# Shifting the state-space inputs by one row: matrix products, or a trip through DRAM

## What is computed

```python
# second token mixer (state space), inside the two-layer network; DIM=512, D_INNER=1024, NHEADS=16, D_STATE=64, CHUNK=64
def ssd_chunk(X, A, Bm, Cm):
    ...                       # S_t = exp(A_t) S_{t-1} + B_t X_t,  Y_t = C_t S_t, written chunk by chunk
zxBCdt = x @ fq4(W_in).T
z = zxBCdt[..., :D_INNER]
x_heads = jax.nn.silu(x_conv).reshape(Bsz, L, NHEADS, HEADDIM)
dt = jax.nn.softplus(dt_raw + dt_bias)
A_disc = -jnp.exp(A_log)[None, None, :] * dt
...                           # rmsnorm, bias and rotation of Bm and Cm
lam = jax.nn.sigmoid(x @ fq4(W_lambda).T)
gamma = lam * dt
beta = (1.0 - lam) * dt * jnp.exp(A_disc)
X = x_heads * gamma[..., None] + jnp.pad(x_heads[:, :-1] * beta[:, 1:, :, None], ((0, 0), (1, 0), (0, 0), (0, 0)))
Y, _ = ssd_chunk(X, A_disc, Bm, Cm)
Y = Y + x_heads * D_param[:, None]
Y = Y.reshape(Bsz, L, D_INNER) * jax.nn.silu(z)
return rmsnorm(Y) @ fq4(W_out).T
```

## Time and profile before

| | |
|---|---|
| median of 3 runs | 3940.6 us (3938.12 to 3940.74) |
| profiled execution | 3943.84 us, its span 3942.0 us |
| TensorE matmul busy | 3380.4 us (86%) |
| VectorE busy | 2652.5 us (67%) |
| ScalarE, GpSimd busy | 1180.4 us (30%), 502.9 us (13%) |
| mean granted TensorE clock | 0.917 of full speed |
| products with `shift` (1227) | 64 records, 32.9 us |
| products with `edge` (1229) | 48 records, 24.5 us |
| token loop of batch 1 | 2785.6 to 2906 us |

### The profile page before, as it was taken

One profiled execution on the slowest core, in us unless ns is written; L12 is line 12 of the kernel. 1 busy time (PEld: TensorE's weight loads), 2 busy tenths in 40 slices (PEclk: granted clock), 3 DMA queues, 4 the chain that ended last, 5 costly groups with the idle time before them and its releaser, 6 DMA issues.

```text
span 3942.0 us, 36808 instructions
## 1 busy us (share of the span) xinstructions
PE 3380.4 (86%) x12493; PEld 2058.3 (52%) x12493; DVE 2652.5 (67%) x3769; ACT 1180.4 (30%) x1948; POOL 502.9 (13%) x404
## 2 busy tenths in 40 slices
PE   1877877877878999999999778898889888988898
PEld 0553653643555777677777435543454346434643
DVE  6877778788785777888888254664566455645563
ACT  1332332332331445334334122212221223123310
POOL 1002002002003111111111112020212011201100
PEclk9888988988989999999999887899889988998799
DMA  3201211211203778787877510132013201220011
GB/s 137 81 24 43 80 34 38 84 34 35 76 23 115 251 246 273 228 275 241 267 269 250 218 53 33 75 112 86 32 75 112 86 32 75 92 106 32 7 58 43
DMA packets 276635, 436.66 MB, mean 111 GB/s; under 512 B 52320, under 2 KB 189536, under 8 KB 263904
## 3 DMA queue, kind: packets, MB, share of 16 engines
q1 hardware_dynamic: 256768, 379.85, 28.5%
q0 software_dynamic: 19680, 54.46, 4.4%
HBM read 364.59 MB, written 93.77 MB: 116 GB/s over the span
## 4 chain that ended last, share of the span: by engine, by line
PE 59%; DVE 24%; DVEq 6%; ACT 5%; issue 3%; DMA 1%; POOL 1%; SPq 0%; ACTq 0%; POOLq 0%
PE bank L1019 11%; PE bank L1048 6%; PE bank L1287 6%; PE bank L1300 4%; PE bank L1308 4%; PE bank L835 3%; PE bank L1216 3%; PE bank L1156 3%; DVE sb_gla L1888 3%; PE bank L1194 2%; DVE sb_ratio L1863 2%; DVEq L1869 2%; PE bank L1025 2%; PE bank L815 2%; PE bank L1252 2%
## 5 line engine op out<-in xcount | busy, mean ns | idle before, releaser
L1019 PE MATMUL bank<-sb_xT,sb_work 128*128 128x256 f32 x2304 | 512.6, 382 | 1.6 <-issue 0.8
L1019 PEld LDWEIGHTS bank<-sb_xT,sb_work 128*128 128x128 f32 x2304 | 438.9, 192 | 75.1 <-issue 17.5
L835 PE MATMUL bank<-sb_gla,sb_work 128*128 128x256 f32 x896 | 261.1, 444 | 111.8 <-DVE sb_work L1890 99.2
L1048 PE MATMUL bank<-sb_work,sb_hT 128*128 128x512 f32 (+1 forms) x666 | 296.1, 592 | 0.0
L835 PEld LDWEIGHTS bank<-sb_gla,sb_work 128*128 128x128 f32 x896 | 189.6, 219 | 174.8 <-DVE sb_work L1890 120.1
L815 PE MATMUL bank<-sb_hT,sb_work 128*128 128x512 f32 x384 | 182.1, 622 | 99.0 <-DVE sb_hT L1837 99.0
L1300 PE MATMUL bank<-sb_parts,sb_gla 128*128 128x512 f32 x512 | 238.8, 610 | 4.5 <-ACT sb_gla L1632 4.1
L1308 PE MATMUL bank<-sb_parts,sb_gla 128*128 128x512 f32 x512 | 230.8, 593 | 6.3 <-DVE sb_work L2469 6.3
L1287 PE MATMUL bank<-sb_work,sb_parts 128*128 128x512 f32 x512 | 231.7, 612 | 2.7 <-ACT sb_work L1645 2.7
L1888 DVE TENSOR_TENSOR sb_gla<-sb_gla,sb_work 128x1024 f32<-128x1024 f32 x112 | 145.9, 1303 | 129.9 <-PE bank L835 124.4
L1156 PE MATMUL bank<-sb_parts,sb_hT 128*128 128x512 f32 x512 | 231.1, 611 | 0.0
(11 more groups left out here) (403 smaller groups left out, 5950.2 us busy)
## 6 DMA issues: line engine op xcount, KB each, us to landing
sb_work<-scratch_gu SPq DMA_DIRECT2D x63, 1408.0 KB
sb_parts<-scratch_mx SPq DMA_DIRECT2D x16, 3072.0 KB, 11.3
sb_work<-moe_w SPq DMA_DIRECT2D x63, 512.0 KB, 6.4
scratch_y<-sb_work SPq DMA_DIRECT2D x48, 512.0 KB, 7.4
sb_parts<-scratch_fq SPq DMA_DIRECT2D x24, 1024.0 KB, 8.0
sb_work<-w_qkvg SPq DMA_DIRECT2D x64, 256.0 KB, 2.4
scratch_gu<-moe_w SPq DMA_DIRECT2D x32, 512.0 KB, 5.8
sb_parts<-fT SPq DMA_DIRECT2D x48, 256.0 KB
```

The costliest lines, as they stand in the source:

```text
L835: mm = pe.matmul(dst.rearrange("p (h n l) -> p h n l", h=HPC, l=size), kS[u % 2][:, k * P:(k + 1) * P], late[:, :, k, :, 1, :], start=True ...
L1019: mm = pe.matmul(dst, egu[j % 3][:, which * NC + k, m * P:(m + 1) * P], xt[j % 2][:, k, :], start=(k == 0), stop=(k == NC - 1))
L1048: mm = pe.matmul(bank(YB[s]), einter[j % 2][0:n, a:a + P], edn[j % 3][0:n, m * D:(m + 1) * D], start=(m == 0), stop=(m == EC - 1))
```

## The change

The products with `shift` and `edge`, the two matrices and the wait for `s_y` ahead of them go. A DRAM tensor `d_late` of 1 + 512 rows is added, whose row 0 GpSimd zeroes once with a DMA at the start. In each batch SyncE stores each finished `xh[k]` one row further on (512 KB), waits for that to land, and loads rows k*128 to k*128+127 back (512 KB), which are the values of the token before; they come into `R[2]` and `R[1]`. These 8 transfers stand in SyncE's queue ahead of the feed-forward loads. VectorE waits once per batch, in tile 0, for all eight, multiplies `late[k]` by beta in place (one instruction of 1024 columns) and adds it.

```diff
--- before.py
+++ after.py
@@ -78,10 +78,6 @@
     parts["ident"] = eye
     parts["ones"] = np.ones((P, P))
     parts["avg_d"] = np.full((P, P), 1.0 / D)
-    parts["shift"] = np.eye(P, k=1)
-    edge = np.zeros((P, P))
-    edge[P - 1, 0] = 1.0
-    parts["edge"] = edge
     head = np.arange(P) // GK
     parts["own_head"] = (head[:, None] == head).astype(np.float32)
     for i in range(NLM):
@@ -146,6 +142,7 @@
     d_gu = nc.dram_tensor("scratch_gu", [NE, P, 2 * NC, EI], F32, kind="Internal").ap()
     d_ids = nc.dram_tensor("scratch_ids", [NE * CAP, 1], U, kind="Internal").ap()
     d_y = nc.dram_tensor("scratch_y", [NSLOT, D], F32, kind="Internal").ap()
+    d_late = nc.dram_tensor("scratch_late", [1 + T, DI], F32, kind="Internal").ap()
     ctx = ExitStack()
     with ctx:
         def sb(name, cols, parts=P):
@@ -351,7 +348,7 @@
         s_v, s_dt, s_cs, s_ang, s_bcn, s_rope, s_tmc, s_cst = series("s_set_dve", 8)
         s_xz = ev("s_xz", NT * 4)
         s_silu = ev("s_silu", NT * 4)
-        s_shift = ev("s_shift", NT)
+        s_late = ev("s_late", 2 * NT, 16)
         s_xg = ev("s_xg", NT)
         s_csb = ev("s_csb", NT * 4)
         s_diff = ev("s_diff", NT * 4)
@@ -492,6 +489,7 @@
 
         X2 = [R[0], xT]
         xb = R[1]
+        late = [R[2 - k // 2][:, (k % 2) * 1024:(k % 2 + 1) * 1024] for k in range(NT)]
         yg = [w(s * 512, 512) for s in range(4)] + [w(14144, 512), small2[:, 2048:2560]]
         yacc = [w(13120 + s * 512, 512) for s in range(2)]
         wzx = big[:, 0:8192].rearrange("p (m c o) -> p m c o", m=4, c=NC)
@@ -771,6 +769,13 @@
                     load_r3(b)
                     sp.wait_ge(x4_ready.sem, x4_ready.at(b - 1, NC))
                     sp.dma_start(out[b - 1], r3(X2[(b - 1) % 2][:, :], T)).then_inc(stored.sem, 16)
+
+                sp.wait_ge(h2_ready.sem, h2_ready.at(b, NT))
+                for k in range(NT):
+                    sp.wait_ge(s_silu.sem, s_silu.at(b, 4 * k + 2))
+                    sp.dma_start(d_late[1 + k * P:1 + (k + 1) * P, :], xh[k]).then_inc(s_late.sem, 16)
+                    sp.wait_ge(s_late.sem, s_late.at(b, 2 * k + 1))
+                    sp.dma_start(late[k], d_late[k * P:(k + 1) * P, :]).then_inc(s_late.sem, 16)
 
                 for ib in range(FB):
                     s = ib % 2
@@ -1220,14 +1225,6 @@
 
                 for k in range(NT):
                     t = slice(k * P, (k + 1) * P)
-                    if k:
-                        pe.wait_ge(s_y.sem, s_y.at(b, k))
-                    for h in range(2):
-                        col = slice(h * 512, (h + 1) * 512)
-                        mm = pe.matmul(bank(h), cst("shift"), xh[k][:, col], start=True, stop=(k == 0))
-                        if k:
-                            mm = pe.matmul(bank(h), cst("edge"), xh[k - 1][:, col], start=False, stop=True)
-                    mm.then_inc(s_shift.sem, 1)
                     if k:
                         pe.wait_ge(s_state.sem, s_state.at(b, k))
                     cs_bcast(k, 0)
@@ -1655,6 +1652,8 @@
                 pool.memset(x, 0.0)
             pool.drain()
             pool.dma_start(d_ids.rearrange("(p n) o -> p (n o)", p=P), zeros.bitcast(U)).then_inc(ids_zero.sem, 16)
+            pool.dma_start(d_late[0:1, :].rearrange("a (p n) -> (a p) n", n=zeros.shape[1]),
+                           zeros[0:DI // zeros.shape[1], :]).then_inc(ids_zero.sem, 16)
 
             for b in range(NB):
                 if b:
@@ -1671,7 +1670,7 @@
                         pool.wait_ge(g_d.sem, g_d.at(u - 1, 1))
                     pool.tensor_tensor(qk, qS[u % 2], kS[u % 2], ALU.mult).then_inc(g_pool.sem, 1)
                 if b == 0:
-                    pool.wait_ge(ids_zero.sem, 16)
+                    pool.wait_ge(ids_zero.sem, 32)
                 pool.wait_ge(m_slot.sem, m_slot.at(b, 1))
                 for i in range(NTK):
                     tk = b * NT + i // TOPK
@@ -2143,7 +2142,7 @@
                 route(b)
                 last = b == NB - 1
                 if b == 0:
-                    dve.wait_ge(ids_zero.sem, 16)
+                    dve.wait_ge(ids_zero.sem, 32)
                 for j in range(ST):
                     dve.wait_ge(m_silu.sem, m_silu.at(b, j + 1))
                     dve.wait_ge(m_up.sem, m_up.at(b, j + 1))
@@ -2398,13 +2397,12 @@
                     differences(0)
 
                     x = Xg[k % 2]
-                    dve.wait_ge(s_shift.sem, s_shift.at(b, k + 1))
-                    for h in range(2):
-                        tt(r3(Xd[:, h * 512:(h + 1) * 512], SP_), r3(bank(h), SP_),
-                           bcast(tm[:, k, 1, h * 8:(h + 1) * 8], SP_), ALU.mult)
+                    if k == 0:
+                        dve.wait_ge(s_late.sem, s_late.at(b + 1, 0))
+                    tt(r3(late[k], SP_), r3(late[k], SP_), bcast(tm[:, k, 1, :], SP_), ALU.mult)
                     dve.drain()
                     dve.wait_ge(s_gx.sem, s_gx.at(b, k + 1))
-                    tt(x, x, Xd, ALU.add).then_inc(s_xg.sem, 1)
+                    tt(x, x, late[k], ALU.add).then_inc(s_xg.sem, 1)
                     differences(1)
                     masked(0)
                     differences(2)
```

## The result

The changed kernel takes 3951.56 us (median of 8 runs, 3946.19 to 3957.27) against 3940.67 (8 runs, 3937.68 to 3949.44): a ratio of 1.0027, 95% interval 1.0016 to 1.0039. So it is slower by about 11 us, where 3938.2 and "no change" were forecast as likeliest. The profiled execution has a span of 3948.1 us and a mean granted clock of 0.912 (before: 3942.0 and 0.917). VectorE has 12 us more to do (2664.4 us) and TensorE 30 us less (3350.5 us), though 57 us of its products are gone: most of the difference is old work that now takes longer, as the next lines show.

A forecast was written before the change was run, and what follows sets the result against it. TensorE carries 59% of the span, but removed products count only where the next step waits for it. Terms of -0.6 us a batch, -2.4 in four, took 3940.6 to 3938.2 us; range 3925 to 3954.

The forecast's parts named there:

- What bounds, and which products are on the chain: Token loop: removed products count only where TensorE is waited for, so in tiles 0, 2 and 3, not tile 1.
- Tile 0, +0.39 from exclusion: Tile 0: VectorE's beta product with both inputs in SBUF and GpSimd exclude each other, losing 0.39 us.
- Tile 1, +1.24: Tile 1: removal gives 0, but TensorE's clock falls in the new pause and an out_project half takes 1.24 us more.
- Tiles 2 and 3, -1.12 each: Tiles 2 and 3: the exponential comes directly behind its table load and the clock holds, gaining 1.12 us a tile.
- Transfers at 0: The stores and loads of 512 KB land before VectorE can use the data, so they cost 0.
- Sum: Four token loops: +0.39 + 1.24 - 1.12 - 1.12 = -0.6 us a batch, -2.4 us in all.
- rival 2: Tiles 1 to 3: without the products each out_project begins at 1.2 GHz; +3 us a batch, +12, 3953; chance 0.12.
- Rival 3: Tile 0: the last load lands at 2792.9 or later, delaying product and addition 2.46 us; 3957 in all; chance 0.08.

The follow-up runs named there:

- experiment 4: Changed kernel plus two unread 512-column products behind the first broadcast of tiles 1 to 3: 3932.50 us, ratio 0.9978 to the kernel before.
- experiment 8: Changed kernel with early beta products and two unread products, minus each block's store and load: 3918.68 us, against 3916.94 with transfers.
- experiment 1: Kernel before with the 14 shift and edge products taken out and nothing in their place: 3951.65 us, ratio 1.0029.
- experiment 2: Changed kernel with as many unread products as before in their old place in tiles 1 to 3: 3945.32 us, ratio 1.0008 to the kernel before.
- experiment 6: Changed kernel with GpSimd's Dx in tile 0 moved after the two products that follow the addition: 3953.35 us, ratio 1.0035 to the kernel before.

## Why the prediction was wrong, step by step

- **What bounds, and which products are on the chain:** right. In tiles 2 and 3 the exponential moved directly behind its table load (2849.71 + 1.28, then 2851.01), and with the clock up (experiment 4) these tiles gained 1.13 us in the mean.
- **Tile 0, +0.39 from exclusion:** right. Measured +0.4 (once +0.7); the product took 1.97 us and `Dx` 2.88, where 1.9 and 2.8 had been named as signs. The Trainium skill's lock rule ("SBUF — State Buffer", "SBUF: two separate sides") is borne out once more: the product took 1.97 us and the addition 2.77, where such an instruction takes 1.23 alone.
- **Tile 1, +1.24:** right in kind, too small. It lost 1.9 to 2.0. `out_project` took 5.7 to 6.0 us, since the clock stayed at 1.2 GHz for most of it (in batch 1 until about 2827, 4.6 us after its start), and the transposes, said to have room, took 1.98 us and ended 0.1 us after the exponential. The row of 5.08 us that set the term was of a half that began at 1.2 GHz and got 2.4 GHz back sooner, after about 3.3 us (granted clock 0.50 in 2895 to 2898 of before, 0.72 in 2898 to 2901).
- **Tiles 2 and 3, -1.12 each:** this step failed: "TensorE's pause here is 2 us with full work on both sides; I let the clock hold, as in 2818 to 2821". There is no full work on both sides. In the changed kernel `out_project`'s second half is followed by 1.82 us of idle time, 1.10 us of transposes with broadcasts around them, and 1.03 us idle again, and TensorE is busy for 1.25 us of 2848 to 2851. The stretch 2818 to 2821 of before was busy for 1.78, with 3.4 us of `shift` and `edge` products a little ahead of it. The nearer row was 2824 to 2827 of before, busy for 1.22, behind which the clock fell; it was used for tile 1 only. Five of eight `out_project` halves came out at 5.8 to 6.3 us and three at 3.84, so in pauses of this kind the clock went either way; what decides between them is not shown. Instead of -9.0 these eight tiles gave -0.5 in sum. Where the clock held the forecast could come out to the digit: tile 2 of batch 3 is at 28.56 us against 29.69.
- **Transfers at 0:** right, shown by experiment 8. In batch 1 of the changed kernel the last load lands 3.5 us after its issue at 2784.16, ahead of VectorE's product at 2789.25.
- **Sum:** 2.0 in tiles 0, 7.8 in tiles 1 and -0.5 in tiles 2 and 3 are +9.2, against -2.4. It is rival 2 in its mechanism and nearly in its price (+12), though only 9 of its 12 halves were slow. It had a chance of 0.12, though the row that speaks for it fitted tiles 2 and 3 as well as tile 1. What the prediction takes from the Trainium skill, page "TensorE: Matmul & The Clock Gate", section "HAM oscillation — how this bites in real kernels", that idle gaps drop the clock to half, agrees with experiments 1, 2 and 4: 6.1 to 6.5 us for the halves without the products, and 3.84 with unread ones.
- **Rival 3, a slip in its sum:** it takes 1 us off for tiles 1 to 3 once, where its terms give 1.0 a batch. With that its price is 16.8 - 4.0, or 3953.4 us and not 3957. It doesn't touch the outcome, as the transfers cost nothing.

## What to carry to other kernels

Before a matmul is taken out for being unneeded, or moved off the path, look at what TensorE does right before and after it and at the granted clock there: work that bridges a pause can be worth more than it costs. Where a kernel alternates between TensorE and VectorE, try unread products in the waits, sized to end before the wait does; here they gave 1.4% by themselves, on the kernel before as it was. And where GpSimd is busy with SBUF, let VectorE's products have an input in PSUM, or make them when GpSimd is idle: here the latter was worth 3.5 us in each tile 0 (26.2 to 22.75).

## What the runs showed of the hardware

- With two unread products of 512 columns in the pause all 12 first halves of `out_project` took 3.84 us; with two of 16 columns the four of tile 1 took 5.7 to 6.0. In tiles 2 and 3 the products of 512 columns stood in a clock that stayed up, in tile 1 in one that was down and came back at about their end. A half of 32 records that ran at 1.2 GHz for 4.6 us took 6.00 us and not 3.84.
- Single tiles of one and the same kernel differ by over 1 us between batches (28.6 and 30.7 in tile 2 of the changed kernel), with the clock up or down in them. And an edit in tile 0 was followed by slow halves in tiles 2 and 3 (experiment 6), so a total alone can hide what an edit did at its own place.
- VectorE and GpSimd exclude each other by whole instructions in a chain too: two VectorE instructions and two of GpSimd's took turns (1.97, 2.88, 2.77 us instead of 1.23, 1.90, 1.23), so removing work ahead of such a pair can win little or nothing (experiment 1: 2 us removed, 0.55 won).
